# Norms and output moments summed by transposing reduces on VectorE instead of products on TensorE, and the leaky step split between ScalarE and GpSimd

## What is computed

```python
x = x + L0(gn(x), acc)          # log of sums of products of exponentials, weights per position
x = x + L1(gn(x), ...)          # attention within each image, then a layer norm and a leaky step

# L1, for one image; v is (1024, 128)
nf = v / max(norm(v, axis=-1), 1e-12)
A  = softmax(5 * (nf @ adj @ nf.T))            # 1024 x 1024
h  = A @ (v @ aff.T + b)
h  = (h - mean(h)) / sqrt(var(h) + 1e-5) * ln_g + ln_b    # over the 128 channels
h  = where(h >= 0, h, 0.01 * h)
```

## Time and profile before

| | |
|---|---|
| time, median of 3 runs (lowest, highest) | 1119.42 us (1118.21, 1122.18) |
| span of the profiled execution (no other time of it is given) | 1118.2 us |
| busy over the span: PE, DVE, ACT, POOL | 93%, 72%, 82%, 48% |
| share of the chain that ended last: PE, DMA, DVE | 84%, 7%, 4% |

### The profile page before, as it was taken

One profiled execution on the slowest core, in us unless ns is written; L12 is line 12 of the kernel. 1 busy time (PEld: TensorE's weight loads), 2 busy tenths in 40 slices (PEclk: granted clock), 3 DMA queues, 4 the chain that ended last, 5 costly groups with the idle time before them and its releaser, 6 DMA issues.

```text
span 1118.2 us, 19802 instructions
## 1 busy us (share of the span) xinstructions
PE 1034.9 (93%) x7144; PEld 784.9 (70%) x7144; DVE 804.3 (72%) x1385; ACT 911.4 (82%) x1703; POOL 536.2 (48%) x267
## 2 busy tenths in 40 slices
PE   1199999968999999999999999999999999999994
PEld 0055555546887877777777777777777788777772
DVE  7723555578777777777777777777777777777776
ACT  1699999538888888888888888888888888888784
POOL 0044455503355555555555555555555555555543
PEclk9999999969999999999999999999999999999998
DMA  8989999730122222222322222223222222222213
GB/s 358 397 330 403 411 404 406 312 151 19 57 77 77 77 76 77 76 76 76 105 104 96 101 107 96 95 80 100 86 77 77 76 76 76 77 77 77 76 57 115
DMA packets 33421, 159.13 MB, mean 142 GB/s; under 512 B 4268, under 2 KB 4904, under 8 KB 23080
## 3 DMA queue, kind: packets, MB, share of 16 engines
q1 hardware_dynamic: 33320, 157.82, 37.1%
HBM read 136.97 MB, written 20.83 MB: 141 GB/s over the span
## 4 chain that ended last, share of the span: by engine, by line
PE 84%; DMA 7%; DVE 4%; ACT 1%; issue 1%; POOL 1%; SPq 1%; POOLq 0%; ACTq 0%; DVEq 0%
PE PS L1207 22%; PE PS L1208 21%; PE PS L1209 21%; PE PS L1225 5%; DMA Wt<-acc 4%; PE PS L1184 4%; PE PS L1174 4%; PE PS L1219 2%; PE PS L1195 2%; DMA X<-x 2%; DVE st L751 2%; PE PS L1213 2%; DMA NU<-factor_rows 0%; SPq L294 0%; PE PS L1240 0%
## 5 line engine op out<-in xcount | busy, mean ns | idle before, releaser
L928 DVE TENSOR_TENSOR Pl<-PS,Ph 128x512 fp32r<-128x512 f32 x512 | 348.1, 690 | 183.6 <-ACT PS L603 178.7
L602 ACT ACTIVATE Ph<-PS 128x512 fp32r<-128x512 f32 x384 | 235.0, 612 | 94.8 <-PE PS L1209 92.1
L603 ACT ACTIVATE PS<-PS 128x512 f32<-128x512 f32 x512 | 305.7, 611 | 7.9 <-PE PS L1209 7.9
L1207 PE MATMUL PS<-Ph,hh 128*128 128x512 f32 x512 | 206.4, 403 | 0.3 <-DVE Pl L928 0.3
L1208 PE MATMUL PS<-Pl,hh 128*128 128x512 f32 x512 | 200.0, 391 | 0.0
L1207 PE MATMUL PS<-uTh,nTh 128*128 128x512 f32 x512 | 199.9, 390 | 0.0
L1209 PE MATMUL PS<-uTh,nTl 128*128 128x512 f32 x512 | 199.6, 390 | 0.0
L1208 PE MATMUL PS<-uTl,nTh 128*128 128x512 f32 x512 | 199.6, 390 | 0.0
L1209 PE MATMUL PS<-Ph,hl 128*128 128x512 f32 x512 | 199.5, 390 | 0.0
L425 POOL TENSOR_TENSOR hl<-X,hh 128x1024 fp32r<-128x1024 f32 (+1 forms) x33 | 77.2, 2339 | 195.4 <-ACT hh L587 169.1
L408 POOL TENSOR_TENSOR LL<-LL 128x512 f32<-128x512 f32 x64 | 82.6, 1290 | 137.5 <-ACT LL L500 137.5
(11 more groups left out here) (136 smaller groups left out, 1595.5 us busy)
## 6 DMA issues: line engine op xcount, KB each, us to landing
Wt<-acc SPq DMA_DIRECT2D x64, 1024.0 KB, 7.5
out<-X SPq DMA_DIRECT2D x38, 512.0 KB, 2.6
X<-x SPq DMA_DIRECT2D x16, 1024.0 KB, 19.7
SQ<-norm_rows SPq DMA_DIRECT2D x31, 512.0 KB, 3.7
X<-factor_rows SPq DMA_DIRECT2D x31, 512.0 KB, 4.1
NU<-factor_rows SPq DMA_DIRECT2D x31, 512.0 KB, 5.0
X<-out SPq DMA_DIRECT2D x7, 512.0 KB, 5.8
out<-X SPq DMA_DIRECT2D x2, 256.0 KB, 2.4
```

The lines of the kernel that those rows point to most:

```text
L602: act.activation(Ph[:, g % RING, :], sl, ACT.Exp, scale=SHARP)
L603: act.activation(sl, sl, ACT.Exp, scale=SHARP).then_inc(weights_ready, 1)
L928: dve.tensor_tensor(Pl[:, r, :], SL[r], Ph[:, r, :].bitcast(F32), ALU.subtract)\
L1207: pe.matmul(out_, lh, rh, start=start, stop=False)
```

## The change

Norms (from the third image on, `SUMMED = 2`) and output moments (but the last half image's) are no longer made on PE. DVE reduces with a transposing `tensor_reduce`: each 32x32 block is transposed and summed, so that a sum over 32 channels of 1024 positions comes out as 32 partitions x 32 columns in each of four quadrants of partitions. Three copies bring the quadrants together on partitions 0 to 31, a small reduce adds the four. The clamp, roots and Newton steps then work on 32x32 (norms) and 32x64 (moments) in SBUF, and a small transpose gives 32 rows of 32 positions, which the DMA writes as 128-byte pieces. The leaky step `max(y, 0.01 y)` becomes `Relu(0.99 y)` on ACT in place of the affine step, and `0.01 y` and an addition on POOL; DVE's part is gone (the last image keeps it). `CAST` and some places in `k` move.

```diff
-CAST = (3, 7, 11, 14)
+CAST = (0, 3, 11, 14)
+KB = NPOS // 32
+SUMMED = 2
 # SP
-                sp.wait_ge(q_steps, 4 * (b + 1))
-                sp.dma_start(factor_rows[b, :, 0:width(b)].rearrange("t (q n) -> q t n", q=Q), rows_of(b)[0:P:32, :, :])
+                    sp.wait_ge(q_steps, q_before(b + 1))
+                    sp.dma_start(factor_rows[b, :, :].rearrange("t (k i) -> k t i", i=32), q_out).then_inc(q_kept, 16)
 # POOL
             def add_residual(b):
+                pool.wait_ge(steep_done, b + 1)
+                pool.tensor_scalar(fac_of(b), fac_of(b), gcol_flat[:, :], lbc_flat[:, :], ALU.mult, ALU.add)\
+                    .then_inc(flat_done, 1)
+                pool.wait_ge(flat_done, b + 1)
+                pool.tensor_tensor(out_of(b), out_of(b), fac_of(b), ALU.add).then_inc(leaky_done, 1)
                 pool.wait_ge(leaky_done, b + 1)
                 xv = X[:, place(b), :]
                 pool.tensor_tensor(xv, xv, out_of(b), ALU.add).then_inc(residual_added, 1)
 # ACT
+            def steep(b):
+                act.wait_ge(output_centred, b + 1)
+                act.activation(out_of(b), fac_of(b), ACT.Relu, bias=lbc_steep[:, :], scale=gcol_steep[:, :])\
+                    .then_inc(steep_done, 1)
                         if k == 4 and b >= 2:
-                            affine(b - 2)
+                            steep(b - 2)
-                        if k == 8 and b + 2 < B:
+                        if k == (4 if b else 8) and b + 2 < B:
                             norm_roots(b + 2)
 # DVE
+            def quadrants(sums, folds, count):
+                dve.wait_ge(folds, count)
+                for g in (1, 2, 3):
+                    dve.tensor_copy(sums[0:32, g], sums[32 * g:32 * g + 32, 0]).then_inc(folds, 1)
+                dve.wait_ge(folds, count + 3)
+            def norm_sums(b):
...
+                dve.tensor_reduce(n_sums[:, 0, :], ZT[b % 2].rearrange("p (k i) -> p k i", i=32), AX.X, ALU.add,
+                                  apply_transpose=True).then_inc(n2_folds, 1)
+            def norm_total(b):
+                at = 5 * (b - SUMMED)
+                quadrants(n_sums, n2_folds, at + 1)
+                dve.tensor_reduce(n_half, n_sums[0:32].rearrange("p g k -> p k g"), AX.X, ALU.add).then_inc(n2_folds, 1)
+                dve.wait_ge(n2_folds, at + 5)
+                dve.tensor_scalar(n_sum, n_half, NORM_MIN**2, None, ALU.max).then_inc(n2_clamped, 1)
+            def norm_rows_out(b):        # three dependent steps, then a transpose
+                dve.wait_ge(n2_roots, 2 * b + 2)
+                dve.scalar_tensor_tensor(out=n_half, in0=n_sum, scalar=-0.5, in1=n_root, ...)
+                dve.tensor_tensor(n_half, n_half, n_root, ALU.mult)
+                dve.scalar_tensor_tensor(out=n_root, in0=n_half, scalar=1.5, in1=n_root, ...)
+                dve.transpose(n_row, n_root).then_inc(n2_steps, 1)
+            def output_sums(b, e):
+                dve.wait_ge(output_taken, 4 * b + 2 * e + 2)
+                dve.tensor_reduce(q_sums[:, 0, :, e * KH:(e + 1) * KH],
+                                  pairs[b % 2][:, :, half(e)].rearrange("p t (k i) -> p t k i", i=32), AX.X, ALU.add,
+                                  apply_transpose=True).then_inc(q_folds, 1)
+            def output_total(b):
+                quadrants(q_sums, q_folds, 6 * b + 2)
+                dve.tensor_reduce(q_sum, q_sums[0:32].rearrange("p g t k -> p t k g"), AX.X, ALU.add).then_inc(q_folds, 1)
 # inverse_deviations: the same four steps, now on q_sum and q_rows in SBUF, then dve.transpose(q_out, q_rows)
-                        if k == 6 and b >= 2:
-                            leaky(b - 2)
+                        if k == (1 if b else 6) and b + 2 < B:
+                            norm_sums(b + 2)
+                        if k == (2 if b else 7) and b + 2 < B:
+                            norm_total(b + 2)
+                        if k == 6 and b:
+                            output_sums(b - 1, 1)
+                        if k == 7 and b:
+                            output_total(b - 1)
+                        if k == 15 and b < B - 1:
+                            output_sums(b, 0)
-                        if k == 7 and b + 2 < B:
-                            clamp(b + 2)
-                        if k == 8 and b + 2 < B:
-                            inverse_norms(b + 2)
+                        if k == (5 if b else 9) and b + 2 < B:
+                            norm_rows_out(b + 2)
 # PE
-                        if k == 7 and b + 2 < B:
-                            norms(b + 2)
-                        if k == (7 if b < B - 1 else 5) and b:
-                            moments(b - 1)
```

## The result

The changed kernel takes 1264.17 us (median of 4 runs, 1263.47 to 1266.61) against 1118.82: ratio 1.128, 95% interval 1.126 to 1.131. It is slower, as forecast, by 145 us where 101 were predicted; 1264 lies near the upper end of the range.

What follows compares the result with a forecast made beforehand. PE bounds the kernel at 26.67 us a batch; DVE would become the bound at 23.7 + 6.0 + 0.4 = 30.1 us. 28 batches add 96 us, the rest 4: about 1220 us, range 1068 to 1270.

Steps and rivals of the forecast that it cites:

- PE's loss of work: Norm and moment products and slower products behind them leave PE in nearly every batch: 1.63 us, floor 26.67 to 25.04.
- DVE's own sum: DVE's work per batch without holds: 20.7 - 4.75 + 3.4 + 3.6 + 0.75 = 23.7 us.
- rival 2: DVE's transposing sums run at half rate and holds stay small: 27.1 us a batch, 1133 us; chance 0.06.
- The holds: DVE's norm total and norm steps stand still while POOL runs on SBUF: 6.0 us a batch.
- the three cases: DVE's holds: only two-operand instructions 5.2 us; copies and clamp too, copies passing together, 6.0; POOL between copies 7.5.
- the third case: POOL gets its turn after each DVE copy, clamp held, norm steps then find POOL idle: 7.5 us lost.
- What waits behind: ACT's deviation roots at k = 8 wait for DVE, exponentials queued behind: 0.4 us of DVE's time, bounds 0 and 0.9.
- the 30.1 foretold: DVE's need per batch as the new bound: 23.7 + 6.0 + 0.4 = 30.1 us, 3.4 more than before.
- the fast end: Forecast with DVE holds of 5.2 us and no gap at k = 8: period 28.9 us, time 1182 us.
- Rival 1: PE keeps the bound, holds costing DVE under 1.3 us a batch: 25.04 to 25.3 us, 1068 to 1080; chance 0.28.
- Rival 3: Holds cost about PE's gain, half lost in DVE's idle time: DVE 26.2 to 27.0 us, 1105 to 1128; chance 0.05.
- The page's rule: DVE with two SBUF inputs, or in two-port copies and tensor_scalar, is locked out while POOL holds the shared ports.

Runs made afterwards that it cites:

- e8: Changed kernel with reduces for copies, norm roots/steps at k = 6/8, deviation roots/steps at 9/10, `values_upper` at 12, clamp replaced by a fifth summand: 1093.6 us, ratio 0.977.

## Why the prediction was right

- **PE's loss of work** came only in part, and only once little holds DVE: e8's most frequent batch is 25.5 us with PE busy nearly throughout, 1.1 below the 26.67 before, where 1.6 was computed and the floor put at 25.04. Where the other 0.5 us is, no run shows.
- **DVE's own sum** was put at 23.7 us. DVE is busy 29.8 us a batch (377 of 400); less 7.2 of holds that is 22.6, or 23.1 with the 0.5 us of gaps between the small steps, which the forecast's 0.22 a step has in it (16 of them are 3.5 us, not 3.6). The transposing reduce takes 1.23 us, the 1.22 that the plain one gave; rival 2 (half rate) is out. The small steps that nothing holds take 0.18 us each.
- **The holds** were put at 6.0 us and measured 7.2, inside the 5.2 to 7.5 of the three cases. Their places were only partly those named. The copies did not pass together: POOL's L447 got in between the first and second, as in the third case, and the third copy slipped through. The clamp was held 0.8, not 2.4. Of the norm steps only the first is held, not two, because by then POOL's stretch was over. And L1038's 2.1 us were not in the forecast at all: I had the deviation steps fall between the additions and the values' lower part and did not ask when that part starts. Two errors in opposite directions, +2.1 and about -1, made the sum come out near; that it did is partly luck.
- **What waits behind:** ACT's waits for totals were costed at 0.4 us at k = 8 and nothing at k = 4. DVE's gaps are 31.58 - 29.8 = 1.8 us a batch; 0.5 of them lie between the small steps, and 1.3 end with ACT's exponentials, 0.9 more than costed. Holds +1.2, waits +0.9 and DVE's own sum -0.6 are the 1.5 us by which the batch is longer than the 30.1 foretold; over 29 batches that is the 44 us missed. The mis-sized terms are the holds and these waits. (At the fast end the forecast's 1182 leaves out its own +4 for the last batches and the closing; 28.9 us a batch give 1186.)
- **Rival 1** (PE keeps the bound) fails by the PE waits shown above; its condition, that holds stay under 1.3 us, is what e8 brings about, where the first norm step is the last one held, 0.75 us on the mean, and the time comes out at 1094 rather than the 1068 to 1080 worked out for it.
- **Rival 3** (a washout) would have needed half the holds to fall in DVE's idle time; DVE had 1.8 us of it.
- **The page's rule** for copies and tensor_scalar, of which the trace before had no row (the Trainium skill, "SBUF — State Buffer", section "Who interferes with whom"): the trace agrees now. Copies and clamp are held. Reduces, which that section says never contend, are not (175 ns beside the same POOL instructions, in the run with reduces for copies).

## What to carry to other kernels

A small VectorE instruction with two SBUF operands, or a copy or scalar step from SBUF to SBUF, cost up to a whole GpSimd instruction here (2.3 us) where it met one: price it by what runs on GpSimd at its place in the order, and move it, or give it one input stream (a reduce, an operand in PSUM). Such holds move on when one is taken away, so the effect of each fix has to be read from the trace of the next kernel. And when work is moved, ask what it had been filling: an engine that waits in its order can turn the place it leaves into the next bound.

## What was not expected

GpSimd gets its turn between two VectorE copies that have no wait between them; the second copy took 2.33 us for that reason, where 0.18 is its like's time elsewhere. A VectorE step issued 0.15 us behind a GpSimd instruction loses 2.1 us (L1038), one issued just ahead of it (L1035) loses nothing, so 0.2 us in the order decides 2.1 of 31.6 us. GpSimd's one-input step took 1.20 us for 1024 columns, half of a two-input one (2.40).
